# Dense retrieval: the left one-hot rows are multiplied by the depths on POOL instead of DVE

## The reference

```python
q = (x @ Wq_pk).reshape(b, n, P, HEADS, DIM_KEY).transpose(2, 0, 1, 3, 4)
sim = jnp.einsum('pbnhd,pkhd->pbnhk', q, pk_keys)      # two sides of 64 keys, 8 heads
scores, idx = jax.lax.top_k(sim, PK_TOPK)              # 16 best of each side
score = (scores[0][..., :, None] + scores[1][..., None, :]).reshape(b, n, HEADS, 256)
final_scores, pk_idx = jax.lax.top_k(score, FINAL_TOPK)  # 16 best of the 256 sums
final_scores = jax.nn.softmax(final_scores, axis=-1)
...
k = jnp.einsum('bnhk,bnhkd->bnhd', kv_scores, keys_table[ind])
v = jnp.einsum('bnhk,bnhkd->bnhd', kv_scores, values_table[ind])
```

## Time and profile before

| | us |
|---|---|
| median of three runs | 4401.82 (4396.14 to 4404.66) |
| the profiled execution | 4401.02, its span 4399.3 |
| PE busy, share of the span | 3578.5, 81% |
| DVE | 2730.3, 62% |
| ACT | 1390.0, 32% |
| POOL | 360.0, 8% |
| retrieval stage, from first comparison to last W | 240 to 2136 |

### The profile page before, as it was taken

One profiled execution on the slowest core, in us unless ns is written; L12 is line 12 of the kernel. 1 busy time (PEld: TensorE's weight loads), 2 busy tenths in 40 slices (PEclk: granted clock), 3 DMA queues, 4 the chain that ended last, 5 costly groups with the idle time before them and its releaser, 6 DMA issues. The chain is left out here.

```text
span 4399.3 us, 54286 instructions
## 1 busy us (share of the span) xinstructions
PE 3578.5 (81%) x16546; PEld 2034.3 (46%) x16546; DVE 2730.3 (62%) x7378; ACT 1390.0 (32%) x2512; POOL 360.0 (8%) x363
## 2 busy tenths in 40 slices
PE   5528889999999999999799967866678461899777
PEld 4325554544444454444355545543456341344354
DVE  3368878877887888555366641135544456999812
ACT  2203444444444444444232221014232134100023
POOL 1000000000000000000100001202000000344500
PEclk8669999999999999999899987978789575999968
DMA  0102343434343433544000020000000003000000
GB/s 7 53 10 70 93 106 83 98 90 98 82 103 87 94 84 82 116 110 101 21 25 22 22 78 0 0 4 1 13 19 1 0 0 86 14 0 0 0 7 6
DMA packets 140947, 207.80 MB, mean 47 GB/s; under 512 B 35104, under 2 KB 119657, under 8 KB 135469
## 3 DMA queue, kind: packets, MB, share of 16 engines
q1 hardware_dynamic: 140717, 205.03, 19.5%
HBM read 115.66 MB, written 10.03 MB: 29 GB/s over the span
## 5 line engine op out<-in xcount | busy, mean ns | idle before, releaser
L951 PE MATMUL psum<-pk_W,pk_kv 128*128 128x512 f32 (+1 forms) x2560 | 1204.8, 553 | 10.0 <-issue 9.9
L1182 DVE SCALAR_TENSOR_TENSOR pk_W<-psum,pk_E 128x512 f32<-128x512 f32 (+1 forms) x1280 | 811.6, 634 | 440.2 <-ACT pk_E L1049 407.1
L1049 ACT ACTIVATE pk_E<-psum 128x512 f32<-128x512 f32 (+1 forms) x1280 | 708.8, 554 | 1005.0 <-PE psum L941 1001.7
L951 PEld LDWEIGHTS psum<-pk_W,pk_kv 128*128 128x128 f32 x2560 | 466.5, 191 | 173.2 <-issue 27.0
L940 PE MATMUL psum<-pk_stack,pk_spread 128*128 128x512 bf16 (+1 forms) x1280 | 462.4, 361 | 90.0 <-DVE pk_W L1182 54.1
L2642 PE MATMUL psum<-tree_w,tree_x 128*128 128x512 bf16 x1728 | 384.6, 382 | 110.9 <-PEq L120 90.6
L941 PE MATMUL psum<-pk_stack,pk_spread 128*128 128x512 bf16 (+1 forms) x1280 | 460.1, 359 | 0.0
L940 PEld LDWEIGHTS psum<-pk_stack,pk_spread 128*128 128x128 bf16 x1280 | 125.0, 98 | 444.4 <-DVE pk_W L1182 349.2
L2713 DVE COPY_PREDICATED leaf_acc<-leaf_path,psum 128x512 f32<-128x512 uint32 x468 | 310.5, 729 | 5.6 <-PE psum L2642 3.3
L2642 PEld LDWEIGHTS psum<-tree_w,tree_x 128*128 (+1 forms) x1728 | 168.6, 99 | 313.2 <-issue 123.3
L941 PEld LDWEIGHTS psum<-pk_stack,pk_spread 128*128 128x128 bf16 x1280 | 125.7, 98 | 241.9 <-issue 232.1
(11 more groups left out here) (558 smaller groups left out, 4880.9 us busy)
## 6 DMA issues: line engine op xcount, KB each, us to landing
pk_kv<-in_kv SPq DMA_DIRECT2D x40, 2048.0 KB, 7.8
pk_stack<-pk_parts SPq DMA_DIRECT2D x768, 64.0 KB, 2.5
pk_stack<-pk_marks SPq DMA_DIRECT2D x256, 64.0 KB, 2.6
peer_soft_kv<-peer_kept SPq DMA_DIRECT2D x32, 288.0 KB, 2.7
peer_kept<-pk_made SPq DMA_DIRECT2D x32, 256.0 KB, 2.1
tree_weights_x<-in_tree_w SPq DMA_DIRECT2D x32, 256.0 KB, 4.5
pk_stack<-pk_parts SPq DMA_DIRECT2D x192, 32.0 KB, 2.0
dft_cos<-in_cos SPq DMA_DIRECT2D x1, 2596.5 KB
```

The source lines that it names most:

```text
L951: nc.tensor.matmul(ps[:, 4, 0:N], kv[:, k % 2, c, :], W[:, n % 3, 0:N], start=(c == 0), stop=(c == CHUNKS - 1)).then_inc(acc_done, 1)
L1049: nc.scalar.activation(E[:, n % 2, 0:width(k)], ps[:, 2 + n % 2, 0:width(k)], ACT.Exp).then_inc(e_made, 1)
L1182: nc.vector.scalar_tensor_tensor(W[:, n % 3, 0:width(k)], ps[:, n % 2, 0:width(k)], TOP + 0.5, E[:, n % 2, 0:width(k)], ALU.is_gt, ALU.mul ...
```

## The change

The multiply of the left half by `depth16` moves from DVE to POOL (`weight_left`). DVE's comparison now signals `equal_made` and DVE goes on without waiting for it; the empty step where the multiply stood stays, so the comparisons keep their chunks. POOL waits for `equal_made` and `depth_made`, multiplies, and signals `onehots`, on which PE's marks wait as before. Before DVE writes `depth16` again it waits for the last tile's multiplies. POOL's loop over jobs becomes a loop over chunks that issues the multiplies and the old subtraction (`split_lo`) where their inputs come. The hunk with the two new semaphores' names is left out here.

```diff
...
@@ -880,10 +880,30 @@
                 for r in range(TOP):
                     last = nc.gpsimd.memset(inverse[:, r:r + 1], 1.0 / (TOP - r))
                 last.then_inc(consts, 1)
-                for k in range(len(jobs)):
+                def split_lo(k):
                     pool.wait_ge(mid_made, k + 1)
                     nc.gpsimd.tensor_tensor(parts[:, k % 2, 2, 0:width(k)], left[:, 0:width(k)],
                                             parts[:, k % 2, 1, 0:width(k)], ALU.subtract).then_inc(lo_made, 1)
+
+                def weight_left(t, h):
+                    pool.wait_ge(equal_made, HEADS * t + h + 1)
+                    pool.wait_ge(depth_made, t + 1)
+                    nc.gpsimd.tensor_tensor(onehot[:, h % 2, 0, :, :], onehot[:, h % 2, 0, :, :],
+                                            rows_of(depth16[:, h, :], KEYS), ALU.mult).then_inc(onehots, 1)
+
+                for t in range(GROUP_TILES[0]):
+                    for h in range(HEADS):
+                        weight_left(t, h)
+                split_lo(0)
+                for n in range(len(jobs) * CHUNKS):
+                    k, c = n // CHUNKS, n % CHUNKS
+                    t, i = slot_of(n)
+                    if t is not None:
+                        for h in range(HEADS):
+                            if i == ONEHOTS_AT + 2 * h + 1:
+                                weight_left(t, h)
+                    if k + 1 < len(jobs) and c == turn_at(k) + 4:
+                        split_lo(k + 1)
 
             @block.tensor
             def _(pe):
@@ -1129,16 +1149,17 @@
                         if a in (2, 8):
                             yield
                     steps.settle()
-                    steps.do(nc.vector.tensor_tensor(depth16[:, :, :], depth[:, :, :], rows_of(inverse[:, :], HEADS), ALU.mult))
+                    if t:
+                        dve.wait_ge(onehots, HEADS * t)
+                    nc.vector.tensor_tensor(depth16[:, :, :], depth[:, :, :], rows_of(inverse[:, :], HEADS), ALU.mult).then_inc(depth_made, 1)
                     for h in range(HEADS):
                         if HEADS * t + h >= 2:
                             dve.wait_ge(marks_made, HEADS * t + h - 1)
-                        steps.do(nc.vector.tensor_tensor(onehot[:, h % 2, :, :, :],
-                                                         idf[:, :, h, :].unsqueeze(2).to_broadcast([P, 2, KEYS, TOP]),
-                                                         count64[:, :, :].unsqueeze(1).to_broadcast([P, 2, KEYS, TOP]), ALU.is_equal))
+                        nc.vector.tensor_tensor(onehot[:, h % 2, :, :, :],
+                                                idf[:, :, h, :].unsqueeze(2).to_broadcast([P, 2, KEYS, TOP]),
+                                                count64[:, :, :].unsqueeze(1).to_broadcast([P, 2, KEYS, TOP]), ALU.is_equal
+                                                ).then_inc(equal_made, 1)
                         yield
-                        nc.vector.tensor_tensor(onehot[:, h % 2, 0, :, :], onehot[:, h % 2, 0, :, :],
-                                                rows_of(depth16[:, h, :], KEYS), ALU.mult).then_inc(onehots, 1)
                         yield
                     dve.wait_ge(exped, t + 1)
                     if t == first_tile[g] and g:
```

More of the change, by code:

```diff
@@ L803, in dense_rows_stage @@
         made = at.sb("made", [P, 2, BANK])
-        (consts, spread_made, xc_made, pk_made, pk_copied, sims_made, sims_copied, shifted, exped, summed, logged,
+        (equal_made, depth_made, consts, spread_made, xc_made, pk_made, pk_copied, sims_made, sims_copied, shifted, exped, summed, logged,
          onehots, marks_made, marks_copied, split, normal, turned, hi_made, left_made, mid_made, lo_made, x_made, e_made,
          w_made, acc_done, acc_copied, vec) = (at.sem(n) for n in (
-            "consts", "spread_made", "xc_made", "pk_made", "pk_copied", "sims_made", "sims_copied", "shifted", "exped",
+            "equal_made", "depth_made", "consts", "spread_made", "xc_made", "pk_made", "pk_copied", "sims_made", "sims_copied", "shifted", "exped",
             "summed", "logged", "onehots_made", "marks_made", "marks_copied", "logits_made", "logits_normal", "logits_turned", "hi_made",
```

## The result

| | median us | runs | ratio to before, 95% interval |
|---|---|---|---|
| before | 4399.84 | 4 | |
| changed kernel | 4456.43 | 4 (4445.15 to 4459.48) | 1.0123, 1.0103 to 1.0144 |

The change makes the kernel 56 us slower, 1.2%; the forecast was 4456 us. The profiled execution was the fastest of the four, 4445.15 us with a span of 4443.4. Of the 44 us by which its span is longer, the retrieval stage holds 53, and the rest of the program was 9 us shorter in this one execution. In the ten traces of this document the rest takes 2495 to 2508 us, whatever the change. So the terms are compared inside the stage.

A forecast was written before the change was run, and what follows sets the result against it. PE was taken to bound at width 512, PE and DVE both near full at 256. Terms 22.2 + 26.4 + 4.8 + 2 = 55.4 us on 4401.0 gave 4456 us, range 4430 to 4496.

The forecast's parts named there:

- POOL's time for the multiply: One 128x1024 bf16 multiply on POOL: 2.14 us from the subtraction rows, with 1.0 and 3.0 kept as bounds.
- Exclusion of the two engines: A two-SBUF-input DVE instruction and a POOL instruction reading SBUF exclude each other, so comparison and multiply run serially.
- Place A: Two tiles before the loop, 16 heads: 11.1 us lost a tile, 22.2 us in all.
- The turns: Serial time per head: held comparison 1.09, POOL's pick-up 0.08, multiply 2.14, together 3.31 us; costs only where longer than before.
- rival 3: Clock falls in the four width-256 tiles because PE is busy only 72%: 35 us more, 4491; chance 0.08.
- Place B: Four tiles inside the loop at width 256, 32 heads: 6.6 us lost a tile, 26.4 us in all.
- Place C: Twelve tiles at width 512, 96 heads: only head 0 short, 4.8 us, plus 2 for POOL's subtraction among the multiplies.
- The cover: At width 512 PE takes 3.57 us a head, above the serial 3.31, leaving 0.26 us to spare.
- the wait after each comparison: DVE's wait that the edit removes; the 98 us taken off DVE give back nothing at width 512, where PE bounds.
- 1: Rival: DVE and POOL overlap after all, leaving a two-buffer circle; 30 us, 4431; chance 0.10.
- 2: Rival: the multiply is far dearer on POOL, 2.9 us; 143 us, 4544; chance 0.09.
- 4: Rival: not slower, POOL streams bf16 at the copy's rate, 1.0 us a multiply; 4402; chance 0.06.

The follow-up runs named there:

- e3: Changed kernel with POOL's multiply replaced by an equally long fill that reads nothing from SBUF; 4433.6 us, ratio to before 1.0079.
- e6: Changed kernel with POOL multiplying only at width 512, plus one two-operand POOL instruction behind each of those 96 multiplies; 4425.4 us, ratio to before 1.0052.
- e7: Changed kernel with POOL multiplying only at width 512, plus one POOL fill behind each of those 96 multiplies; 4397.0 us, ratio to before 0.9987.
- e8: Changed kernel with 3 more PE products ahead of each head's marks in the two opening tiles; 4455.1 us, ratio to before 1.0116.
- e2: Changed kernel with POOL multiplying only in the two opening tiles, DVE in the others; 4420.2 us, ratio to before 1.0052.
- e5: Changed kernel with all 144 multiplies back on DVE, keeping only the moved wait; 4395.7 us, ratio to before 0.9983.

## Why the prediction was right

Point by point, by its own steps.

- **POOL's time for the multiply:** 2.14 us from the line through two subtractions, 2.12 measured. Right. (Its upper bound was worked out wrongly: half as much again as 2.36 is 3.5, not 3. Nothing in the sum hangs on it.)
- **Exclusion of the two engines:** shown, by more than the two meetings. Each of the 28 held comparisons at B ends 1.08 to 1.09 us after POOL's multiply; e3 took the reading away and no comparison was held by what stood in its place; e6 and e7 add an instruction of about the same length, and only the one that reads costs. That the two engines hold each other over a tile that both use is excluded by e6 and by the earlier trace rows, where the tiles differ. The Trainium skill's rule ("SBUF — State Buffer", section "Who interferes with whom") holds here for reading; that a POOL instruction which only writes doesn't contend with a two-input DVE instruction, which the same section says, e3 and e7 bear out.
- **Place A:** 24.8 against 22.2. The turns were right: the first tile's last multiply ended at 264.97, 26.2 us after the first comparison started (26.4 forecast). The missing 2.6 us are put down to the clock between the tiles. PE idled ahead of each head's marks (1.35 us ahead of the last), the granted clock was 0.50, and the last marks (1.93 instead of 1.23), the projections and the score products that follow took together 3.4 us longer. e8 doesn't undo that, so the cause is read from the trace and not shown by a run. The prediction had put this effect at B (rival 3), where the clock stayed at 0.99 (366 to 600 us).
- **Place B:** 26.4, as forecast, turn 3.28. The mechanism was right; the agreement to a tenth is luck, for the four tiles lost between 5.9 and 8.1 us each where 6.6 was forecast.
- **Place C:** 1.6 against 6.8. The cover held. The term was mis-sized twice. The step that cost the edit "the wait after each comparison" at nothing failed: C is 2.0 to 2.3 us shorter where the wait is gone and POOL has no multiply there (e2 and e5). POOL's part is then about 3.8, less than the 6.8 of head 0 and the subtractions together. At head 0 the prediction had 0.12 us for the semaphore and 0.15 for the weight load behind the multiply; the marks of 808.91's tile start 0.15 us behind it in all, 3.57 us after the comparison and 0.27 later than before instead of 0.4. Its sign that comparisons at C would last about 1.22 us held for two in three only: 30 of the 96 were held, at little cost, since PE sets the pace.
- **The sum:** 52.9 in the stage against 55.4. That the median lies within 1 us of the forecast owes something to chance: the changed kernel's four executions lie 14 us apart, and the rest of the program 13 us over the ten traces.
- **The rivals:** 1 is excluded, since comparisons are held, but its working describes e3 (30 us, 28.8 measured in the stage). 2 and 4 are excluded by the 2.12 us. 3 didn't occur at B.

## What to carry to other kernels

Before work goes from DVE to POOL, look in the trace for a DVE and a POOL instruction that both read two operands and meet: if one ends late by the other's rest, as here, add their times up as one engine's, and compare that turn with what the slowest engine takes for the same piece of work. Where the turn is shorter (C, 3.28 under 3.58), the move costs little (some 4 us in 1463) and gives nothing; where it is longer, each piece pays the difference. When a change bundles a move with a removed wait, try the wait alone: here it was the only part that paid.

## What the runs showed that was not expected

- W behind an unneeded wait for the comparison ahead of it starts 0.12 us later (medians 1.25 and 1.13 us after the comparison's start). Taking this wait off the 128 W that had it gave 6 us in all (e5).
- When POOL's multiply ended in e6, the comparison issued at 858.67 went ahead of POOL's next instruction, issued at 859.57. That fits "first issued, first served"; the other order, POOL waiting longer than DVE, isn't shown here.
- With PE's gaps filled, the granted clock over the first tile's 27 us was 0.85 instead of 0.50, and over the next 38 us 0.52 (e8). A higher clock for the marks alone was worth 1 us.
- POOL multiplies 512 columns of bf16 by bf16 in the 1.157 us that it takes for float32 less bf16.
